# State-space cross-attention block with routed experts: output tiles spread over more slots, layer-norm scale and shift in two buffers

## What is computed

```
state = state * exp(delta * A) + (delta * u) * B
y     = sum over the 16 states of state * C
y     = (y + D * u) * silu(layernorm(x))
x1    = x + y
```

## Time and profile before

| | |
|---|---|
| median of three runs | 2501.58 us (2497.5 to 2501.91) |
| the profiled execution | 2498.76 us, span 2496.7 us |
| VectorE busy | 2120.9 us, 85% of the span |
| TensorE matmuls busy | 2029.5 us, 81% |
| ScalarE busy | 1602.5 us, 64% |
| GpSimd busy | 1445.0 us, 58% |
| mean granted TensorE clock | 0.897 |

### The profile page before, as it was taken

How to read it: one execution, slowest core, us unless ns; L and a number is a source line. 1 busy time by engine, 2 the same in 40 slices (tenths; PEclk the granted TensorE clock), 3 DMA queues, 4 the chain that set the end, 5 groups by cost and what they waited for, 6 DMA issues and landing times.

```text
span 2496.7 us, 32788 instructions
## 1 busy us (share of the span) xinstructions
PE 2029.5 (81%) x10840; PEld 1208.8 (48%) x10840; DVE 2120.9 (85%) x2692; ACT 1602.5 (64%) x2357; POOL 1445.0 (58%) x993
## 2 busy tenths in 40 slices
PE   6798888986757997995757897897776897895899
PEld 2677676654433553453443454454443454453244
DVE  5889799979998999989999899999998899994310
ACT  2677786656768869655658868755666768752500
POOL 0688677767756655656766665665675566663000
PEclk9899989997879999997878998998777998898799
DMA  5311424554603844565621654565541264566411
GB/s 172 128 35 51 155 92 157 181 178 161 236 26 105 293 133 147 171 211 191 231 81 68 232 192 134 165 194 194 199 169 64 77 216 154 183 216 240 171 59 67
DMA packets 200186, 382.76 MB, mean 153 GB/s; under 512 B 31537, under 2 KB 97073, under 8 KB 200018
## 3 DMA queue, kind: packets, MB, share of 16 engines
q1 hardware_dynamic: 196848, 380.21, 45.6%
q10 hardware_dynamic: 3170, 0.47, 0.1%
HBM read 346.53 MB, written 34.08 MB: 152 GB/s over the span
## 4 chain that ended last, share of the span: by engine, by line
PE 44%; DVE 19%; issue 18%; ACT 13%; POOL 3%; DMA 2%; SPq 1%; DVEq 0%; ACTq 0%; POOLq 0%
PE dense L1079 13%; PE dense L906 9%; DVE h L1447 8%; PE dense L844 5%; ACT dA L1190 4%; PE dense L892 3%; DVE dense L1423 3%; POOL h L813 2%; DVE u L1301 2%; PE dense L856 2%; PE dense L865 2%; ACT L1157 2%; PE dense L1056 2%; PE dense L1009 2%; PE dense L913 2%
## 5 line engine op out<-in xcount | busy, mean ns | idle before, releaser
L813 POOL TENSOR_TENSOR h<-h,Cb 128x1024 f32<-128x1024 f32 x512 | 1208.3, 2360 | 429.3 <-DVE h L1447 405.7
L1190 ACT ACTIVATE dA<-delta,Av 128x512 f32<-128x512 f32 x1024 | 703.3, 717 | 383.9 <-DVE h L1447 380.3
L906 PE MATMUL dense<-ident,h 128*128 128x128 f32 x4096 | 605.2, 299 | 161.0 <-POOL h L813 159.4
L906 PEld LDWEIGHTS dense<-ident,h 128*128 128x128 f32 x4096 | 521.1, 155 | 312.4 <-POOL h L813 218.5
L1447 DVE TENSOR_TENSOR_SCAN h<-dA,state,dense 128x512 f32<-128x512 f32 x512 | 627.3, 1262 | 31.6 <-issue 15.2
L1447 DVE TENSOR_TENSOR_SCAN h<-dA,dense 128x512 f32<-128x512 f32 x512 | 596.8, 1203 | 22.9 <-PE dense L906 9.7
L1423 DVE TENSOR_TENSOR dense<-dense,Bb 128x512 f32<-128x512 f32 x864 | 550.3, 682 | 1.6
L1079 PE MATMUL dense<-w3h,xT 128*128 128x512 f32 x832 | 386.4, 598 | 0.0
L807 POOL COPY state<-h 128x2 f32<-128x2 f32 x256 | 47.6, 186 | 337.3 <-DVE h L1447 335.8
L892 PE MATMUL dense<-Bb,duT 128*128 128x128 f32 x1280 | 180.5, 289 | 41.5 <-DVE h L1447 32.1
L844 PE MATMUL dense<-ctxs,win 128*128 128x512 f32 x432 | 208.4, 627 | 2.1 <-ACT szT L1222 1.5
(11 more groups left out here) (153 smaller groups left out, 2061.2 us busy)
## 6 DMA issues: line engine op xcount, KB each, us to landing
sww<-in_sw SPq DMA_DIRECT2D x170, 512.0 KB, 4.3
Cb<-bc_scratch SPq DMA_DIRECT2D x64, 512.0 KB, 6.0
Bb<-bc_scratch SPq DMA_DIRECT2D x54, 512.0 KB, 4.5
w3h<-in_sw SPq DMA_DIRECT2D x54, 512.0 KB, 7.7
w3h<-in_w3T SPq DMA_DIRECT2D x52, 512.0 KB, 4.8
row<-x_scratch SPq DMA_DIRECT2D x42, 512.0 KB, 4.6
xz<-in_x SPq DMA_DIRECT2D x64, 256.0 KB, 4.8
xt<-in_x SPq DMA_DIRECT2D x64, 256.0 KB, 4.0
```

The lines of the kernel that those rows point to most:

```text
L813: e.tensor_tensor(h[:, s:s + 2, :], h[:, s:s + 2, :], Cb[:, 2 * q:2 * q + 2, :], ALU.mult).then_inc(prod_done, 1)
L906: mm = e.matmul(yT[:, k, :], h[:, 2 * ((PAIRS * g + q) % RH) + i, k * P:(k + 1) * P], ident[:], is_transpose=True, start=False, stop=(q == ...
L1190: e.activation(dA[:, i % RA, :], delta[:, st % 2, :], ACT.Exp, scale=Av[:, j * N + n:j * N + n + 1]).then_inc(dA_done, 1)
```

## The change

1. In batches 1 and 2 (`SPILL`) the 32 parts of u = 0 are spread over 31 slots from slot 56 (to 86), and `hidden` of u = 1 starts at slot 91 with 9/4 slots between items. The 32 parts of u = 1 begin at slot 109, one in each slot, so the last 13 (slots 128 to 140) fall into slots 0 to 12 of the next batch, with the last three `tile_out` in slots 6, 10 and 13 and one in slot 2. `tile_out` stands two slots behind its last part (one for the last tile). The rows for u = 1 are loaded at slots 68, 70, 79, 82, normalized at 74, 77, 82, 85 and turned at 77, 80, 84, 88. The logits of batches 1 and 2 take 5 slots for each row block (before 8, 8, 8, 12) and are normalized in slots 91, 96, 102, 107. With the ring of three, some weight tiles are now issued in the slot in which they are used.
2. The items `tile`, `tile_out`, `w3_load` and `res_load` carry the batch that they belong to (`fb`), since they can stand in another one. Batch 3 and the tail keep their places.
3. `r1` and `nm1`, scale and shift, have two buffers by `b % 2`, and GpSimd's wait at line 752 is for the batch before the last. `ln1_rstd` and `ln1_shift` stand 5 and 7 slots behind the load of the last block: slots 69 and 71 in batches 1 and 2, 45 and 47 in batch 0.
4. `ln1_stats` of batch 0 stand in slots 8, 13, 18, 23, 28, 33, 38 and 43 (that is q = 0, 5, 2, 7, 4, 1, 6, 3 of steps 1 to 5), with the loads three slots ahead.
5. `b1s` and `b2s`, two columns, share a tile with `minus_half`.

```diff
+SPILL = (1, 2)
...
         for b in range(NB):
-            self.logits(b, rows, list(range(TB)), [80, 83, 95, 103], [83, 91, 99, 109], [8, 8, 8, 12], RING_B)
+            if b in SPILL:
+                self.logits(b, rows, list(range(TB)), [86, 90, 97, 102], [88, 93, 99, 104], [5] * TB, RING_B)
+            else:
+                self.logits(b, rows, list(range(TB)), [80, 83, 95, 103], [83, 91, 99, 109], [8, 8, 8, 12], RING_B)
...
     def add(self, b, t, *what):
+
+        if b < NB and t >= STEPS * SLOTS:
+            b, t = b + 1, t - STEPS * SLOTS
         self.slots[b][t].append(what)
...
             for k in range(J):
-                rows.append((b, 54 + 3 * k // 2, "ln1", k))
-                self.add(b, 57 + 3 * k // 2, "ln1_stats", k)
-            self.add(b, 124, "ln1_rstd")
-            self.add(b, 126, "ln1_shift")
+                t = 54 + 3 * k // 2 if b else 5 + 5 * k
+                rows.append((b, t, "ln1", k))
+                self.add(b, t + 3, "ln1_stats", k)
+            self.add(b, t + 5, "ln1_rstd")
+            self.add(b, t + 7, "ln1_shift")
...
+        spill = b in SPILL
         for k in range(TB):
-            t = [72, 75, 78, 80][k]
-            rows.append((b, [66, 68, 74, 77][k], "turn", k))
-            self.add(b, [70, 72, 77, 80][k], "renorm", k)
+            t = ([77, 80, 84, 88] if spill else [72, 75, 78, 80])[k]
+            rows.append((b, ([68, 70, 79, 82] if spill else [66, 68, 74, 77])[k], "turn", k))
+            self.add(b, ([74, 77, 82, 85] if spill else [70, 72, 77, 80])[k], "renorm", k)
...
-        for u, hidden, tiles, span in ((0, 39, 56, 23), (1, 83, 99, 28)):
+        for u, hidden, pace, tiles, span in ((0, 39, 8, 56, 31), (1, 91, 9, 109, 32)) if spill else ((0, 39, 8, 56, 23), (1, 83, 8, 99, 28)):
             for hp in range(J):
-                t = hidden + 2 * hp
+                t = hidden + pace * hp // 4
...
-                        self.add(b, at[m + c], "tile", u, dh, k, c)
-                    self.add(b, at[m + W3C - 1] + 2 if at[m + W3C - 1] < 126 else 127, "tile_out", u, dh, k)
+                        self.add(b, at[m + c], "tile", b, u, dh, k, c)
+                    last = at[m + W3C - 1]
+                    self.add(b, last + 1 + (m + W3C < len(at)) if spill else min(last + 2, 127), "tile_out", b, u, dh, k)
...
-        r1 = sb("r1", [P, J])
-        nm1 = sb("nm1", [P, J])
+        r1 = sb("r1", [P, 2, J])
+        nm1 = sb("nm1", [P, 2, J])
...
-                e.wait_ge(zn_done, 1 + STEPS * b)
+                e.wait_ge(zn_done, 1 + STEPS * max(b - 1, 0))
...
-                        uu, dh, k, part = a
-                        bank = bank_of(b, "tile", uu, dh, k)
-                        w3, loaded, value = w3_of(b, uu, dh, part)
+                        fb, uu, dh, k, part = a
+                        bank = bank_of(fb, "tile", uu, dh, k)
+                        w3, loaded, value = w3_of(fb, uu, dh, part)
```

More of the change, by code:

```diff
@@ L90, in __init__ @@
                     for name, bank in self.banks(b, what, args):
-                        self.use[(b, *name)] = (bank, uses[bank])
+                        key = name[1:] if what == "tile" else name
+                        key = (key[0], what, *key[1:]) if what == "tile" else (b, *key)
+                        self.use[key] = (bank, uses[bank])
                         uses[bank] += 1
     def add(self, b, t, *what):
+        if b < NB and t >= STEPS * SLOTS:
+            b, t = b + 1, t - STEPS * SLOTS
         self.slots[b][t].append(what)
@@ L206, in tail @@
                 for k in range(TB):
-                    self.add(b, t - 7, "res_load", u, dh, k)
+                    self.add(b, t - 7, "res_load", b, u, dh, k)
                     for c in range(W3C):
-                        self.add(b, t, "tile", u, dh, k, c)
-                    self.add(b, t, "tile_out", u, dh, k)
+                        self.add(b, t, "tile", b, u, dh, k, c)
+                    self.add(b, t, "tile_out", b, u, dh, k)
                     t += 4
@@ L244, in banks @@
             return [((what, *args), F0 if args[0] else F2)]
-        if what == "tile" and args[3] == 0:
-            return [((what, *args[:3]), F0 + (TB * args[1] + args[2]) % 2)]
+        if what == "tile" and args[4] == 0:
+            return [((what, *args[:4]), F0 + (TB * args[2] + args[3]) % 2)]
         return []
@@ L275, in build @@
         iota = sb("iota", [P, E])
-        minus_half = sb("minus_half", [P, 1])
+        small = sb("small", [P, 3])
+        minus_half, b1s, b2s = small[:, 0:1], small[:, 1:2], small[:, 2:3]
         xpw = sb("xpw", [P, J, DR + 2 * N])
@@ L1070, in slot @@
                                 last = ("expert_out", uu, J - 1)
-                                e.wait_ge(evac[bank_of(b, *last)], 1 + count(b, *last) + 1)
-                            e.wait_ge(evac[bank], 1 + count(b, "tile", uu, dh, k))
+                                e.wait_ge(evac[bank_of(fb, *last)], 1 + count(fb, *last) + 1)
+                            e.wait_ge(evac[bank], 1 + count(fb, "tile", uu, dh, k))
                             for n in range(QD // P):
@@ L1405, in slot @@
                     elif what == "tile_out":
-                        uu, dh, k = a
-                        bank = bank_of(b, "tile", uu, dh, k)
-                        n = part_index(b, uu, dh, k, 0) // W3C
-                        e.wait_ge(part_done, 1 + part_index(b, uu, dh, k, W3C - 1) + 1)
+                        fb, uu, dh, k = a
+                        bank = bank_of(fb, "tile", uu, dh, k)
+                        n = part_index(fb, uu, dh, k, 0) // W3C
+                        e.wait_ge(part_done, 1 + part_index(fb, uu, dh, k, W3C - 1) + 1)
                         e.wait_ge(res_loaded[n % 2], 1 + 16 * (n // 2 + 1))
```

42 lines of the change are left out of this document (20 added, 22 removed).

## The result

The changed kernel takes 2505.11 us (median of 20 runs, 2497.93 to 2509.39). The kernel before took 2497.77 us in 20 runs on the same chips. The ratio is 1.0031, with a 95% interval of 1.0024 to 1.0038: slower by 0.3%, where I had forecast 0.6% faster. The profiled execution took 2508.26 us, 3.1 us above the median of its own kernel.

The account below looks back on a forecast made before the run. VectorE was busy in 85% of the span, with TensorE the bound from 846 to 918 us of batch 1. Batch 0 at 0, batches 1 and 2 -20.7, spill +6.0 sum to -14.7 us: 2487 us, range 2472 to 2504.

Parts of the forecast that it names:

- Tiles of u = 0: Spread over 31 slots in batches 1 and 2, VectorE's waits of 2.22, 1.81 and 1.02 us go: -5.05 us a batch.
- Expert work of u = 1: From slot 91, gelu, a normalization and silu never all meet; half the gaps of slots 86 to 94 go: -2.1 us.
- Last tile: Tiles of u = 1 from slot 109: the last tile's 2.52 us wait behind a projection at slot 126 goes: -2.5 us.
- logit tile: Logits leave slots 112 to 124, so the 5.87 us chain before the new B and C loses one tile: -0.6 us.
- Shift: Moved to slot 71, waits for GpSimd go and it takes 1.2 us: -2.1 in batches 1 and 2, -4.5 in batch 0.
- Weight ring: Ring of three with less lead, some tiles issued in their slot of use: +2.0 us a batch, bounds 0 to 6.0.
- Spill: Slots 11 to 16 of batches 2 and 3: SP issues w3h's routing tiles late, delaying TensorE and VectorE: +3.0 us each.
- Statistics of batch 0: ScalarE blocks in new slots cost +8.3 us by their q, old places give back -3.8; with the shift, batch 0 is 0.
- The signs that I had named for a wrong forecast: Batches 1 and 2 shorter by less than 5 us each, or steps 1 to 5 of batch 0 over 12 us longer.
- The waits only move: Rival, 2502 us, chance 0.20: crowd re-forms at slots 96 to 107 (+4.2), ring +8.0 for two, blocks +2.7.
- SP's order: Rival, 2514 us, chance 0.12: SP's queue becomes the bound in slots 11 to 13 of batches 2 and 3 and the ring.
- The clock falls: Rival, 2511 us, chance 0.06: spilled parts run at TensorE's low clock in a batch's first step, +24 us in two batches.

Follow-up runs that it names:

- odd slots: Changed kernel with all eight hidden items of u = 1 every two slots from 91 to 105, not 9/4 apart: 2483.81 us, ratio 0.9945.
- the version with the old statistics: Changed kernel with the statistics of batch 0 back in their old slots 57 to 67, spill and early shift kept: 2504.2 us, ratio 1.0024.
- the kernel before on even slots: Kernel before with the hidden items of u = 1 at slots 82, 84, 86 to 96 instead of 83 to 97: 2520.21 us, ratio 1.0097.
- the shift alone: Kernel before with only the two buffers and the early scale and shift, no spill, statistics of batch 0 in old slots: 2498.84 us, ratio 1.0007.
- the statistics at every eighth slot: Changed kernel with hidden items on odd slots and batch 0's statistics at slots 10, 18, to 66: 2480.72 us, ratio 0.9939.

## Why the prediction was wrong, step by step

**Tiles of u = 0** (forecast -5.05 us a batch). The three waits went, as forecast, and TensorE's load fell. But "no waits on line 1079 at slots 64 to 80" did not hold. Overlooked was the end of the row: the last part stands in slot 86 behind a projection of 3.60 us, and the new rule puts its addition in slot 87, one slot behind where it was two. The new wait of 3.11 us and the 1.87 at slot 64 take back what was won. One slot more recovered 3.3 us.

**Expert work of u = 1** (forecast -2.1). This is the step that failed: "never all three. I take half: -2.1 us". I asked only where `gelu`, a normalization and silu meet, and gave no heed to the slots of the hidden layers themselves. `9 * hp // 4` moves four of them to even slots, one of them the slot of the projection. Instead of a gain this costs 10.3 us in each batch: 3.5 for hp = 4 and 5, the rest for hp = 6 and 7. With odd slots batch 1 is 13.1 us shorter. 2.8 of these are four additions of 0.69 us that moved to the next batch; that the other 10.3 are what the sum gave for a batch is luck. By the rows the tiles of u = 0 gave 0.1 there instead of 5.05, the expert work 3.0 (4.17 gone, 1.22 new) instead of 2.1, the shift 1.0 instead of 2.1, the ring cost 0 instead of 2.0, and 3.4 came from the wait of softplus in slot 124, which the sum does not have. In batch 2 the odd order is worth 8.5.

**Last tile** (-2.5) and **logit tile** (-0.6). Right in batch 1: the 2.52 us wait is gone, and the 5.87 us one is 5.28. But I counted batch 1 twice, and in batch 2 the last tile had waited only 1.10 us. "Gap for gap" was not so: the 1.96 us of slot 94 is missing there too.

**Shift** (-2.1 a batch, -4.5 in batch 0). The wait of 0.99 us went, but the duration in batches 1 and 2 did not fall to 1.2 us. VectorE of the changed kernel, the shift of each:

```profile
874.01 2.30 DVE L1321 SCALAR_TENSOR_TENSOR nm<-mv,r 128x8 f32<-128x8 f32 x1
...
1461.10 2.32 DVE L1321 SCALAR_TENSOR_TENSOR nm<-mv,r 128x8 f32<-128x8 f32 x1
```

GpSimd's product began at 873.93 us and took 2.36, so both end together again, as in the earlier trace rows. I had the shift 1.3 us into that product, but GpSimd makes the scale just before it, and so the product starts when the shift can. The term was thus -1.0 at most and not -2.1. By itself the move gained nothing in the time of the old order, since the tile behind it waits for TensorE. In batch 0 it freed 5.6 us in step 15 and paid 2.65 + 0.17 at slot 47, where it waited for GpSimd again. "It has no such delay before it" was false there; I had written it for slots 69 and 71, and batch 0 has 45 and 47.

**Weight ring** (+2.0). It cost 0, my low end.

**Spill** (+3.0 each). Right in place and nearly in size. The waits that I named are there in batch 2: TensorE for `w3h`, ScalarE's copy behind it, and VectorE at the recurrence of slot 16. The three engines in order of time:

```profile
1201.64 0.64 PE L1067 MATMUL dense<-w3h,row 128*32 128x256 f32 x8 [1.88 <-DMA w3h<-in_sw]
1203.10 1.06 PE L1067 MATMUL dense<-w3h,row 128*32 128x256 f32 x8 [0.82 <-DMA w3h<-in_sw]
...
1209.49 1.08 ACT L1275 COPY xT<-dense 128x512 f32<-128x512 f32 x2 [1.81 <-PE dense L997]
...
1211.27 2.33 DVE L1458 TENSOR_TENSOR_SCAN h<-dA,dense 128x512 f32<-128x512 f32 x2 [0.85 <-ACT dA L1201]
```

The loads came 2.7 us late instead of 4 and the recurrence 0.85 instead of 2.2, but the addition at slot 13 waited 2.03 instead of 0.8, and a tap 1.38. Steps 0 to 2 of batch 2 are 6.4 us longer, of which 2.8 are the moved additions; so 3.6 us, and 3.5 in batch 3.

**Statistics of batch 0** (+8.3 for the blocks, -3.8 for the old places). The 13.1 us of steps 0 to 5 hold 2.8 us of the shift, so the blocks cost 10.3 against the version with the old statistics, 2.0 more than I had. The 12.7 us of steps 6 to 12 hold 4.3 of the shift at its place in that version, which leaves 8.4. Of these only 4.8 lie in steps 7 and 8, where the old blocks stand, near my 3.8; the other 3.6 lie in steps 6, 10 and 11, which have no block in either version, and are not explained. Step by step, step 1 (slots 8 and 13) cost 3.3 us, as I had it. Steps 2 and 4 cost 4.6 and 3.7 where I had 2.2 each, and there the granted clock was 0.83 (134 to 165 and 192 to 223 us) against 1.00 and 0.94 in the version with the old statistics. What I left out is TensorE's clock. How much of it the blocks bring is open, for a step of 30.1 us at 0.83 stands without any block in the kernel before (step 3, against 27 us at 0.94 elsewhere). VectorE and TensorE of the changed kernel behind the block of slot 8:

```profile
108.20 0.75 DVE L1312 SCALAR_TENSOR_TENSOR u<-dense,cw,u 128x511 f32<-128x511 f32 x1 [3.79 <-ACT u L1127]
```

```profile
114.04 1.92 PE L917 MATMUL dense<-ident,h 128*128 128x128 f32 x8
```

The sum of a pair of states (eight matmuls) took 1.92 us there, and 1.04 at the full clock. The stage table has the granted clock at 0.68 from 106 to 122 us, where it was 1.00 before:

```profile
106.00:122.00 16.00, 11.12 (x53) 8.78 (x52) 11.61 (x14) 10.87 (x19) 10.14 (x8) 0.68 0.11 30
```

The block is not the only cause of this either: with the old statistics the same stretch has 0.79, and step 1 is 2.6 us longer than before with no block in it.

**The sum.** Batch 0 came out at +1.1 (with the 3.1 us of step 3 set right) where I had 0. Leaving out the moved additions (2.8 us each way), batches 1 and 2 with their own new order came to 0.0 and +1.8 us where I had -10.3 each, and the spill to 3.6 and 3.2 where I had 3.0 each. That is +9.7 against -14.7, and the 20.6 us of even slots are most of the difference of 24.4; the medians differ by +7.3. The signs that I had named for a wrong forecast came: batch 1 is 2.8 us shorter and batch 2 longer, and steps 1 to 5 of batch 0 are 12.9 us longer (16 with step 3 set right). The base was off as well: the first three runs had 2501.58 us where twenty have 2497.77, and this alone put the forecast 3.8 us too high.

**The rivals.** *The waits only move* named the right form, a crowd that forms again at 96 to 107, but priced it at 4.2 us for both batches; it is 20.6. That its 2502 us is near the measured 2505.11 is luck, since 8.0 of its terms are for the ring, which cost nothing. *SP's order* did not become the bound. *The clock falls* did not happen where I had put it: in the first 32 us of batch 2 the granted clock rose from 0.69 to 1.00, with TensorE busy for 26.97 us, and a part took 1.88 us. The Trainium skill, page "TensorE: Matmul & The Clock Gate", part 1, has the low clock as the resting state that activity lifts; the row agrees. It was low around slots 9 and 102 instead.

**Order and clock in slot 102.** The trace of the kernel before on even slots tells the two apart. In slot 94 of batch 1 the order is the same: the projection waits for the silu, `hidden` stands behind it, and VectorE's addition behind that.

```profile
986.55 3.67 PE L844 MATMUL dense<-ctxs,win 128*128 128x512 f32 x8 [2.19 <-ACT szT L1222]
990.16 1.13 PE L999 MATMUL dense<-xT,w1s 64*128 64x512 f32 x4
```

```profile
995.14 0.75 DVE L1403 SCALAR_TENSOR_TENSOR xT<-dense,b2s,xT 128x512 f32<-128x512 f32 x1 [1.83 <-PE dense L1009]
```

The granted clock was 1.00 there from 986 to 994 us, the projection took 3.67 us, and the addition waited 1.83 us. In slot 86 of batch 2 of that run it is between the two:

```profile
1535.12 5.23 PE L844 MATMUL dense<-ctxs,win 128*128 128x512 f32 x8 [3.02 <-ACT szT L1222]
```

```profile
1545.25 0.75 DVE L1403 SCALAR_TENSOR_TENSOR xT<-dense,b2s,xT 128x512 f32<-128x512 f32 x1 [3.39 <-PE dense L1009]
```

In all three, with the 6.73 and 4.89 us of the changed kernel, the wait is the projection's time less 1.84 us. By this comparison the order makes 1.83 of the 4.89 us, against 1.22 on the odd slot, and the low clock the other 3.06. TensorE's idle time does not by itself bring the low clock: after 2.19 us of it the projection took 3.67 us, after 2.43 us in the changed kernel 6.73.

**Left open.** What makes the clock fall in slot 102 in both batches is not shown. Nor was it tried whether hp = 6 or hp = 7 alone makes the stalls of slots 107 to 112; that the wait at slot 112 goes with the odd placing is shown, its chain was only read. The steps 5 to 7 that are 4 to 5 us longer in some executions without an edit have no explanation either.

## What to carry to other kernels

When a change states the places of work in a formula, write out every place and lay it over the fixed pattern of the engines (here q of the slot: projection, softplus, silu, normalization), not only over the work that seems to be in conflict. A wait that leaves an engine is a gain only if what it does next is not itself waiting for another engine; ask this of the next instruction on the row. Before two items of a chain through a shared bank are moved closer, count the slots from the one that fills the bank to the one that empties it.

## What the runs showed that I had not expected

- One digit in the pace of eight small items (a hidden layer is 1.13 us of TensorE) is worth 21 us of 2500.
- A shift on 128 x 8 elements took 0.14 us with GpSimd idle, 0.17 us where a copy of 0.18 us stood on GpSimd between the scale and the next product (slot 47 of batch 0), and 2.30 to 2.32 us where the product had begun 0.06 to 0.08 us before the shift. In the four traces that were read for it (both kernels, the shift alone, the statistics at every eighth slot) there is nothing between.
- The same stretch of TensorE's work has different clocks in different executions of the same order: step 3 of batch 0 took 30.1 us at 0.83 in the kernel before, and 26.9 at 0.94 in its version with even slots, which has no edit there.
- The changed kernel's runs spread over 11.5 us (2497.93 to 2509.39), those of the kernel before over 6.2.
